# Layer 3's attention: its first two chunks prepared inside the feed-forward stage ahead of it

## What is computed

```python
x = x + 0.5 * ffn(layernorm(x))     # layer 3, feed-forward (first call)
x = x + attn(layernorm(x))          # layer 3, attention
x = x + 0.5 * ffn(layernorm(x))     # layer 3, feed-forward (second call)

def ffn(x):                         # 128 -> 512 -> 512 -> 512 -> 128
    h = silu(x @ w1.T * s1) * (x @ w2.T * s2)
    h = gelu(h @ h1.T * s3)
    h = gelu(h @ h2.T * s4)
    return h @ w3.T * s5

def attn(x):                        # 16 sequences of 256 tokens, 16 heads of 8
    q, k, v = heads(x @ W_q.T), heads(x @ W_k.T), heads(x @ W_v.T)
    p = softmax(q @ k.T / sqrt(8))
    return merge(p @ v) @ W_o.T
```

## Time and profile before

| | us |
|---|---|
| median of three runs | 3030.87 |
| lowest, highest of the three | 3022.91, 3030.93 |
| the profiled execution's own time | 3022.15 |
| its span, first to last instruction | 3020.3 |
| PE busy in the span | 2316.6 (77%) |
| DVE busy in the span | 1769.5 (59%) |
| mean granted TensorE clock | 0.848 of full |

### The profile page before, as it was taken

How to read it: one execution, slowest core, us unless ns; L and a number is a source line. 1 busy time by engine, 2 the same in 40 slices (tenths; PEclk the granted TensorE clock), 3 DMA queues, 4 the chain that set the end, 5 groups by cost and what they waited for, 6 DMA issues and landing times. The chain is left out here.

```text
span 3020.3 us, 46343 instructions
## 1 busy us (share of the span) xinstructions
PE 2316.6 (77%) x14088; PEld 1672.9 (55%) x14089; DVE 1769.5 (59%) x4313; ACT 1064.8 (35%) x2478; POOL 850.1 (28%) x770
## 2 busy tenths in 40 slices
PE   4979959668366730775999971675999688899998
PEld 3645546447354710663676650564877445557877
DVE  5758957563566358822333349824565568765565
ACT  1433324431143110452444422452333145563332
POOL 2535425438213820672000010673000122201000
PEclk9989959865686565997999985898999679999999
DMA  6110011336413674453000026453000233310000
GB/s 205 39 58 1 1 41 41 116 129 145 132 66 131 145 226 42 105 121 100 1 2 0 1 87 95 98 121 77 0 0 1 67 76 86 83 36 1 0 0 28
DMA packets 274629, 204.04 MB, mean 68 GB/s; under 512 B 102432, under 2 KB 253453, under 8 KB 271405
## 3 DMA queue, kind: packets, MB, share of 16 engines
q1 hardware_dynamic: 240301, 168.05, 20.1%
q0 software_dynamic: 34176, 34.09, 6.9%
HBM read 136.20 MB, written 64.91 MB: 67 GB/s over the span
## 5 line engine op out<-in xcount | busy, mean ns | idle before, releaser
L161 POOL TENSOR_TENSOR fields<-ln_t,power 128x4 f32<-128x4 f32 x96 | 98.4, 1051 | 604.8 <-DVE ln_t L154 604.8
L3051 DVE TENSOR_REDUCE s_mx<-s_sa 128x2 f32<-128x512 f32 x256 | 166.8, 685 | 59.0 <-PE s_sa L3204 57.5
L3132 ACT ACTIVATE s_e<-s_sc 128x512 f32<-128x512 f32 x256 | 149.6, 599 | 119.2 <-PE s_sc L3220 117.4
L2788 PE MATMUL s_z<-s_t,s_mix_h 128*128 128x256 f32 x768 | 171.0, 379 | 0.0
L1996 POOL DMA_INDIRECT acc_dram<-s_yo,s_to_i x96 | 152.4, 1588 | 46.7 <-issue 27.8
L1984 POOL DMA_INDIRECT s_xg<-rows_dram,s_from_i x96 | 94.5, 985 | 223.2 <-DVE s_to_i L2117 195.2
L2788 PEld LDWEIGHTS s_z<-s_t,s_mix_h 128*128 128x128 f32 x768 | 145.9, 190 | 19.8
L190 PE MATMUL s_tp<-ident,xn 128*128 128x128 f32 x224 | 46.4, 344 | 135.6 <-DVE xn L180 133.8
L3204 PE MATMUL s_sa<-s_kx,s_qx 72*128 72x256 bf16 x512 | 110.7, 303 | 38.2 <-DVE s_mx L3051 20.5
L2406 DVE TENSOR_SCALAR s_den<-s_kn 128x8 f32<-128x8 f32 x64 | 10.3, 161 | 208.4 <-PE s_kn L2567 208.4
L2301 PE MATMUL s_hu<-s_xgt,s_w 128*128 128x128 f32 x768 | 118.0, 300 | 7.8 <-issue 6.9
(11 more groups left out here) (516 smaller groups left out, 6189.5 us busy)
## 6 DMA issues: line engine op xcount, KB each, us to landing
s_w<-in_L_ffn_W_dram SPq DMA_DIRECT2D x96, 256.0 KB
acc_dram<-s_zero SPq DMA_DIRECT2D x32, 512.0 KB, 5.8
s_kx<-k_dram SPq DMA_DIRECT2D x16, 576.0 KB
s_qx<-q_dram SPq DMA_DIRECT2D x48, 192.0 KB
fields<-acc_dram SPq DMA_DIRECT2D x16, 512.0 KB, 7.5
table_dram<-s_table_rows SPq DMA_DIRECT2D x2, 3136.0 KB, 9.2
s_wg<-in_L_ffn_w_gate_dram SPq DMA_DIRECT2D x64, 96.0 KB
s_wu<-in_L_ffn_w_up_dram SPq DMA_DIRECT2D x64, 96.0 KB
```

The source lines that it names most:

```text
L161: pool.tensor_tensor(core.rstd[:, tiles], core.ln_t[:, 2, tiles], core.power[:, 0:CT], ALU.pow).then_inc(s.scale_ready.sem, 1)
L2788: last = pe.matmul(bank(n)[:, o, :], weights[:, f, o * P:(o + 1) * P], src[:, f, :], start=f == 0, stop=f == HALF - 1)
L3051: dve.tensor_reduce(mx[:, i, t, 2 * pairs:2 * pairs + 2], sa[:, n % 2, :, :], AX.X, ALU.max).then_inc(max_done.sem, 1)
L3132: act.activation(e[:, n % RING, :, :], sc[:, n % 2, :, :], ACT.Exp).then_inc(exp_done.sem, 1)
```

## The change

Chunks 0 and 1 of attention are normalised, and their keys and queries projected, split and stored, in rounds 6 and 7 of the first `l3_ffn`. Their rows of `x` are final by then. The attention stage begins with the load of sequence 0, ahead of its weights. The positions `at` below lie between the seven products of a layer; `c` is the round, `k` the layer in it, `a` (0 or 1) the attention chunk, `n` is 0 for keys and 1 for queries.

```diff
@@ l3_ffn
+            @block.sync
+            def _(sp):
+                for n, m in enumerate(("W_k", "W_q")):
+                    sp.dma_start(raw_a[n], w[f"L3_attn_{m}"]).then_inc(aw_loaded.sem, 16)
+                for a in range(EARLY):
+                    for n in range(2):
+                        sp.wait_ge(a_split_done.sem, a_split_done.past(2 * a + n))
...
+                                sp.dma_start(core.k_dram[2 * a + i].rearrange("a d h t -> (d h) a t"), cut).then_inc(a_stored[0].sem, 16)
...
+                                    sp.dma_start(core.q_dram[2 * a + i, :, k, :, :], cut[:, k, :]).then_inc(a_stored[1].sem, 16)
+                sp.wait_ge(a_stored[0].sem, 32 * EARLY)
+                sp.wait_ge(a_stored[1].sem, 32 * TERMS * EARLY)
@@ l3_ffn, gpsimd
+                pool.wait_ge(a_var_ready.sem, 1)
+                for c in range(EARLY):
+                    tiles = slice(c * CT, (c + 1) * CT)
+                    pool.tensor_tensor(core.rstd[:, tiles], core.ln_t[:, 2, tiles], core.power[:, 0:CT],
+                                       ALU.pow).then_inc(a_scale_ready.sem, 1)
@@ l3_ffn, vector: early(c, k, at) is called at 0, 2, 3, 4, 5, 6 of each layer
+            def early_normal(a, tiles=range(CT)):
+                dve.wait_ge(a_scale_ready.sem, a_scale_ready.past(a))
...
+            def early_left(a, n):
+                dve.wait_ge(a_first_cut.sem, a_first_cut.past(2 * a + n))
+                dve.scalar_tensor_tensor(left[n], s.tp[:, 0, :], SCALE if n else 1.0, parts[:, n, 0, :],
+                                         ALU.mult, ALU.subtract).then_inc(a_left_ready.sem, 1)
+            def early_last(a, n):
+                dve.wait_ge(a_second_cut.sem, a_second_cut.past(2 * a + n))
+                dve.tensor_tensor(parts[:, n, 2, :], left[n], parts[:, n, 1, :], ALU.subtract).then_inc(a_split_done.sem, 1)
+                a = c - (CHUNKS - EARLY)
+                if a == 0 and k == 0:
+                    if at == 0:
+                        early_scales()
+                    if at == 3:
+                        early_normal(0, range(2))
+                    if at == 4:
+                        early_normal(0, range(2, CT))
+                if (a, k) in ((0, 1), (1, 0)):
+                    if at == 2:
+                        early_left(a, 0)
+                    if at == 4:
+                        early_last(a, 0)
+                    if at == 5:
+                        early_left(a, 1)
+                if a == 0 and k == 1 and at == 6:
+                    early_last(0, 1)
+                if a == 1 and k == 1 and at == 0:
+                    early_last(1, 1)
@@ l3_ffn, scalar: after the copy (0) and after each gelu (1 to 4)
+                if a == 0 and k == 0 and at == 1:
+                    act.wait_ge(aw_turned.sem, 1)
...
+                if a == 0 and k == 1 and at == 0:
+                    early_xnt(0)
+                if (a, k) in ((0, 1), (1, 0)):
+                    if at == 1:
+                        early_cut(a, 0)
+                    if at == 2:
+                        early_cut2(a, 0)
+                    if at == 3:
+                        early_cut(a, 1)
+                    if at == 4:
+                        early_cut2(a, 1)
@@ l3_ffn, tensor: early(c, k, at) is called after products 1, 2, 5 and 6 of each layer
+                if a == 0 and k == 0 and at == 1:
+                    pe.wait_ge(aw_loaded.sem, 32)
+                    pe.wait_ge(s.xnt_ready.sem, s.xnt_ready.past(c + 1))
+                    for n in range(2):
+                        last = pe.transpose(s.tp[:, 0, n * P:(n + 1) * P], raw_a[n], core.ident[:, :])
+                    last.then_inc(aw_turned.sem, 1)
+                if a == 0 and k == 0 and at == 6:
+                    early_turn(0)
+                if (a, k) in ((0, 1), (1, 0)):
+                    if at == 2:
+                        early_project(a, 0)
+                    if at == 5:
+                        early_project(a, 1)
@@ l3_ffn, round 7 (there is no next chunk): DVE early_normal(1), ACT early_xnt(1), PE early_turn(1)
+                elif first:
+                    early_turn(1)
@@ l3_attn, sync
-            for m in names:
-                sp.dma_start(raw[m][:, :], w[f"L3_attn_{m}"]).then_inc(w_loaded.sem, 16)
+            load(0, 0, 0, False)
+            for m in names:
+                sp.dma_start(raw[m][:, :], w[f"L3_attn_{m}"]).then_inc(w_loaded.sem, 16)
+            load(0, 0, 1, False)
             sp.wait_ge(ones_ready.sem, 1)
...
-            store(0, 0)
-            load(0, 0, 0, False)
-            load(0, 0, 1, False)
-            store(1, 1)
             load(1, 1, 0, False)
@@ l3_attn, vector
+            ln_scales_dve(dve, core, s)
+            ln_dve(dve, core, s, 0, 0)
+            ln_dve(dve, core, s, 1, 1)
             dve.memset(ones[:, :], 1.0).then_inc(ones_ready.sem, 1)
...
-            split(0, 0)
-            split(0, 1)
-            split(1, 0)
-            split(1, 1)
-            dve.wait_ge(v_clear.sem, 2)
-            keep_v(0, 0)
             for n in range(STEPS):
                 largest(0, 0, n)
             split_maxima(0)
+            dve.wait_ge(v_clear.sem, 2)
+            keep_v(0, 0)
@@ l3_attn, scalar and tensor
-                keep(c, 0)
-                keep(c, 1)
...
-            project(0, 0, 0)
-            pe.wait_ge(pj_kept.sem, pj_kept.past(0))
-            project(0, 0, 1)
             ln_pe(pe, core, s, 1, 1)
-            pe.wait_ge(pj_kept.sem, pj_kept.past(1))
-            project(1, 1, 0)
...
-            project(1, 1, 1)
-            pe.wait_ge(pj_kept.sem, pj_kept.past(3))
             project_v(0, 0)
```

More of the change, by code:

```diff
@@ new lines, in early @@
+            def early(c, k, at):
+                if not first or not isinstance(c, int):
+                    return
+                a = c - (CHUNKS - EARLY)
[17 more added lines that the diff above has]
+                    early_last(1, 1)
@@ L2762, in _, with early_xnt, early_cut, early_cut2 @@
             ln_act(act, core, s, 0, 0)
+            def early_xnt(a):
+                act.wait_ge(a_turned.sem, a_turned.past(a))
+                act.activation(xta, s.tp[:, 0, :], ACT.Copy).then_inc(a_xnt_ready.sem, 1)
+            def early_cut(a, n):
+                act.wait_ge(a_projected.sem, a_projected.past(2 * a + n))
+                if a:
+                    act.wait_ge(a_stored[n].sem, (32, 32 * TERMS)[n] * a)
+                act.activation(parts[:, n, 0, :], s.tp[:, 0, :], ACT.Copy, scale=SCALE if n else 1.0).then_inc(a_first_cut.sem, 1)
+            def early_cut2(a, n):
+                act.wait_ge(a_left_ready.sem, a_left_ready.past(2 * a + n))
+                act.activation(parts[:, n, 1, :], left[n], ACT.Copy).then_inc(a_second_cut.sem, 1)
+            def early(c, k, at):
+                if not first or not isinstance(c, int):
+                    return
+                a = c - (CHUNKS - EARLY)
+                if a == 0 and k == 0 and at == 1:
+                    act.wait_ge(aw_turned.sem, 1)
+                    for n in range(2):
+                        last = act.activation(wt_a[n].rearrange("p (d h) -> p d h", h=HEADS),
+                                              s.tp[:, 0, n * P:(n + 1) * P].rearrange("p (h d) -> p d h", d=DH), ACT.Copy)
+                    last.then_inc(aw_kept.sem, 1)
+                if a == 0 and k == 1 and at == 0:
[9 more added lines that the diff above has]
+                        early_cut2(a, 1)
             def body(c, u, more=True):
@@ L2783, in _, with early_turn, early_project, early @@
             ln_pe(pe, core, s, 0, 0)
+            def early_turn(a):
+                pe.wait_ge(a_xn_ready.sem, a_xn_ready.past(a))
+                if a:
+                    pe.wait_ge(a_left_ready.sem, a_left_ready.past(2 * a - 1))
+                else:
+                    pe.wait_ge(aw_kept.sem, 1)
+                for j in range(CT):
+                    last = pe.transpose(s.tp[:, 0, j * P:(j + 1) * P], xa[:, j, :], core.ident[:, :])
+                last.then_inc(a_turned.sem, 1)
+            def early_project(a, n):
+                if n:
+                    pe.wait_ge(a_left_ready.sem, a_left_ready.past(2 * a))
+                else:
+                    pe.wait_ge(a_xnt_ready.sem, a_xnt_ready.past(a))
+                pe.matmul(s.tp[:, 0, :], wt_a[n], xta, start=True, stop=True).then_inc(a_projected.sem, 1)
+            def early(c, k, at):
+                if not first or not isinstance(c, int):
+                    return
+                a = c - (CHUNKS - EARLY)
+                if a == 0 and k == 0 and at == 1:
+                    pe.wait_ge(aw_loaded.sem, 32)
+                    pe.wait_ge(s.xnt_ready.sem, s.xnt_ready.past(c + 1))
+                    for n in range(2):
+                        last = pe.transpose(s.tp[:, 0, n * P:(n + 1) * P], raw_a[n], core.ident[:, :])
[7 more added lines that the diff above has]
+                        early_project(a, 1)
```

(2 more changed lines are left out.)

105 lines of the change are left out of this document (80 added, 25 removed).

## The result

| | before | after |
|---|---|---|
| median of 9 runs each, us | 3030.79 | 3016.74 |
| lowest to highest | 3022.91 to 3040.41 | 3006.19 to 3027.85 |
| the profiled execution's own time | 3022.15 | 3016.74 |
| its span | 3020.3 | 3015.2 |
| mean granted clock | 0.848 | 0.847 |

The ratio is 0.9956 with a 95% interval of 0.9936 to 0.9975: 0.44% faster, and the medians lie 14.05 us apart. The changed kernel's is already 2.0 us ahead when the changed stage begins (PE's first transposes at 2079.72 against 2081.74), which is none of the change's doing.

A forecast was written before the change was run, and what follows sets the result against it. PE was taken to bound the feed-forward stage and a chain of waits attention's start. Gains of 15.9 and 2.8 less 4.6 us gave 14.1 us, so 3016.8 us off the median, range 3004 to 3024.

The forecast's parts named there:

- The cost: Feed-forward rounds 6 and 7: inserted PE transposes and products add 4.6 us, all on the path; DVE, ACT and POOL nothing.
- the gaps ahead of DVE's additions: DVE within a feed-forward layer: gaps up to 1.0 us before most additions, each large enough for one inserted 0.69 us operation.
- The first score: Attention's start: the first row score comes 15.9 us earlier, at 2385.4 instead of 2401.3, limited next by the weights.
- the weights' delay: Attention's start: weights queued behind sequence 0's load on SP's queue land no earlier than it, at 2379.5, instead of after 3.3 us.
- The bounds of that term: Attention's start: the weights' landing was kept between 2378.6 and 2380.4, making the total gain 15.0 to 13.2 us.
- The loop's begin: Start of attention's loop: PE goes on 5.6 us after the maxima's split instead of 8.4, `place_nm` hidden; gain 2.8 us.
- The sum: Whole run: 15.9 + 2.8 - 4.6 = 14.1 us faster, 3016.8 us off the three runs' median.
- two levels 8 us apart: Whole run: times of one kernel lie at two levels 8 us apart, and the range must hold both.
- the first rival: Attention's start: the weights are not held back, taking their old 3.3 us; total gain 19.2 us, 3011.7; chance 0.08.
- the second: Feed-forward rounds 6 and 7: six hand-offs come a 1.0 us gap late, 6 us lost, 3022.8; chance 0.16.
- The third: Attention's loop: the half clock lasts three more sequences, the 14 us gain is gone; with five, 3041; chance 0.06.
- the clock came back within two sequences before: Attention's loop: an argument against the clock staying at half, which would cost 4.9 us per further sequence.

The follow-up runs named there:

- e6: Changed kernel with the four inserted float32 products of 128x512 on PE made twice; rounds 6 and 7 took 39.14 and 38.53 us, the profiled run 3026.66.
- e5: Changed kernel with DVE's eight inserted subtractions made twice; rounds 6 and 7 took 37.65 and 36.75 us, the profiled run 3028.56.
- e1: Changed kernel with the four attention weights issued ahead of sequence 0's load; median 3011.47 us, ratio 0.9945 to the kernel before.
- e7: Changed kernel with the four attention weights issued by ACT on its own queue instead of SP; median 3019.73 us, ratio 0.9965 to the kernel before.
- e3: Kernel before with sequence 0's `place_nm` issued ahead of the load of sequence 2 at attention's start; ratio 0.9993, PE went on 3.5 us sooner.
- b1: Kernel before, unaltered, profiled again; it took 3028.54 us.
- b2: Kernel before, unaltered, profiled another time; it took 3031.49 us.
- e8: Changed kernel with POOL beginning the split of chunk c + 2 only after DVE split the maxima in round c's first half; median 3012.85 us, ratio 0.9949.
- e9: Changed kernel with weights ahead of sequence 0's load, POOL's split later, and the loop's `place_nm` ahead of the load; median 2977.51 us, ratio 0.9818.
- e10: Kernel before with only two loop edits, POOL's later split and `place_nm` ahead of the load; median 2997.26 us, ratio 0.988.

## Why the prediction was right

**The cost.** 4.6 us were predicted, with rounds near 37.5 and 36.9; it is 4.5, with 37.43 and 36.82. That PE pays in full is shown by e6, that DVE's part is covered by e5. One reading was wrong and did no harm: the gaps ahead of DVE's additions are not each large enough for 0.69 us. In a layer before the change they are 0.28 or 0.52, 1.04, 1.04, 0.44 and 1.04 us, and an operation put into a small one only shifts the next. ACT's and SP's part was not tested by doubling. The last query stores were issued until 2361.9 and the stage ended at 2369.7, with DVE's last sums as before, so the stores did not hold it.

**The first score.** 15.9 us were predicted and 16.1 came; the parts were 10.9 to the weights (11.1) and 5.9 behind them (5.3, as the second `ln_pe` and `project_v` overlap more than I allowed). That the weights are the limit and the load no longer is, e1 shows. One step was right in size, but its cause is not settled: I put the weights' delay down to their place on SP's queue. e7 took them off it, three of the four landed sooner and the last, on which PE waits too, did not. The bounds of that term were too narrow as well: I kept 10.0 to 11.8, and five traces with the changed kernel's order have 10.6 to 14.9. The Trainium skill's ring order ("DMA: Bandwidth & Descriptors", "Queues, rings and completion order") agrees with e1 and e3; the same section says that an engine alternates between queues, which the first three weights of e7 (1.9 to 7.8 us after the first issue, against 6.8 to 10.1) agree with and the last (12.4 against 11.1) does not look like. The Trainium skill's fit in "Anatomy of one DMA", 2.0 us plus bytes at 436 GB/s, gives 4.7 us for this load as an estimate, and no trace has it. The Trainium skill states it for one DMA issued by GpSimd; the load is four, issued by SP.

**The loop's begin.** 2.8 us were predicted, 2.7 came, with `keep_v` at 0.88 and `place_nm` landing in 1.9. e3 confirms the cause by itself. The size belongs to the trace I had: its first key score comes 8.8 us after the split, those of b1 and b2 7.6 and 7.1, against 6.1 after, so beside them the gain is 1.5 and 1.0.

**The sum.** 14.1 predicted, 14.3 in the steps of the trace, 14.05 in the medians. The forecast on the median was 3016.8, the median is 3016.74; such closeness is luck within a spread of 21.7 us. By the table, from the first key score less the rounds, the gain is 14.7 us against the first trace of the kernel before, 13.7 against b1 and 13.1 against b2. The runs don't lie at two levels 8 us apart, as the range supposed; the nine of the kernel before fill 3022.91 to 3040.41.

**The rivals.** That the weights are held back was right, against the first rival. PE stalls did not appear, against the second. The third, attention at the half clock, has something to it, but not as I put it: the clock does fall in the loop, at a cost of some 6 us each time, in both kernels. What fails is the step "the clock came back within two sequences before": the trace I had was the one of three of that kernel without a later fall. That rival's idle gaps were there too: where they are gone (e8, e9, e10), even the interval of sequences 1 to 2 takes 15.5 to 16.0 us at a granted clock of 1.00, instead of 21.0 to 21.7 at 0.67 or 0.68.

## What to carry to other kernels

Work moved into a stage that one engine fills costs what that engine does in it, and the rest is free as long as the others' gaps hold; both can be tested by doubling one engine's share. At a stage's start, issue small transfers that a chain waits for ahead of large ones (e1, e3); another queue alone did not replace that in e7, where the last of four came no sooner. Take more than one profile before calling a loop's timing the kernel's, and compare kernels that ran on different chips each against the kernel before on its own.

## What the runs showed of the hardware that I had not expected

A small DVE operation on 128x32 elements (0.18 to 0.19 us) takes 0.6 to 1.2 while POOL works through its 1.0 to 1.2 us operations on 128x512. The Trainium skill, "SBUF — State Buffer", section "Who interferes with whom", says that a DVE instruction with two SBUF inputs contends with a GpSimd instruction that reads SBUF, and one in a mode that uses both ports as well; the pair is held for a whole instruction and the other engine waits. The alternation in the timeline agrees for the two operations with two inputs (1.17 us each); the other two have one input (0.61 and 0.91), and no run shows in which mode they ran. The four operations together held PE for 2.8 to 3.2 us in each of six rounds. With these gaps there were up to three falls of PE's clock in a trace, each costing about 6 us and at places that differ from run to run; with the gaps gone (e9, e10) there was none in the same sequences, though the interval of sequences 13 to 14 took 17.8 and 19.5 us there, at 0.87 and 0.82, instead of the usual 15.5 at 1.00. That the gaps are what lets the clock fall is thus borne out but not proved: e8 had other gaps in their stead, at `place_nm`, and no odd-to-even interval above 16.8, yet intervals of 25 us at the new waits.

From the first issue of the 1152 KB load until PE had the weights behind it, the same steps took between 10.6 and 14.9 us in five traces; what makes the slow ones slow stays open.
